# Grouping the eight attention score products of a tile in two groups of four

## What is computed

```python
q, k, v = split(shift_token(x) @ wqkv)        # 8 heads x 64
q = rotary(l2norm(q) * q_scale); k = rotary(l2norm(k) * k_scale)
# windows of 128 rows; each sees its own keys and those of the window before
sim = einsum('bhwid,bhwjd->bhwij', 8 * q, k)  # 128 x 256 per head
attn = softmax(where(mask, -max, sim))
o = einsum('bhwij,bhwjd->bhwid', attn, v)
x = x + o @ wo                                # then layer norm, w1, gelu gate, w2
```

## Time and profile before

| | |
|---|---|
| median of 3 runs | 4835.5 us |
| lowest, highest run | 4827.64, 4853.87 us |
| profiled execution, span on core 0 | 4868.1 us |
| TensorE busy | 4402.9 us, 90% of the span |
| TensorE weight loads busy (beside the products) | 2909.9 us, 60% |
| VectorE busy | 3162.0 us, 65% |
| ScalarE busy | 2817.5 us, 58% |
| GpSimd busy | 1583.5 us, 33% |
| score products, L1328 | 2048 MATMULs, 470 ns each in the mean |
| mean granted TensorE clock | 0.952 of full speed |

### The profile page before, as it was taken

How to read it: one execution, slowest core, us unless ns; L and a number is a source line. 1 busy time by engine, 2 the same in 40 slices (tenths; PEclk the granted TensorE clock), 3 DMA queues, 4 the chain that set the end, 5 groups by cost and what they waited for, 6 DMA issues and landing times.

```text
span 4868.1 us, 84300 instructions
## 1 busy us (share of the span) xinstructions
PE 4402.9 (90%) x28128; PEld 2909.9 (60%) x28128; DVE 3162.0 (65%) x8864; ACT 2817.5 (58%) x5822; POOL 1583.5 (33%) x1700
## 2 busy tenths in 40 slices
PE   8888999996999999999999999999998999999998
PEld 3444444443666666666666666666666666666666
DVE  5666666665666666666666666666666666666665
ACT  6666777674555555555555555555555555555554
POOL 2112211213333333333333333333333334333332
PEclk9999999998999999999999999999999999999999
DMA  1000000002000000000000000000000000000000
GB/s 63 28 28 28 28 19 20 19 19 83 10 9 10 9 9 9 9 10 10 10 9 9 11 9 10 10 9 9 9 9 10 9 9 9 11 9 10 9 9 6
DMA packets 71343, 74.95 MB, mean 15 GB/s; under 512 B 11792, under 2 KB 69776, under 8 KB 70288
## 3 DMA queue, kind: packets, MB, share of 16 engines
q1 hardware_dynamic: 71056, 71.88, 4.7%
HBM read 45.91 MB, written 25.17 MB: 15 GB/s over the span
## 4 chain that ended last, share of the span: by engine, by line
PE 41%; DVE 16%; issue 9%; POOL 8%; ACT 2%; DVEq 1%; DMA 0%; SPq 0%; POOLq 0%; ACTq 0%
PE f_ps L1391 16%; PE f_ps L1401 8%; POOL rnorm L946 8%; PE f_ps L1302 6%; PE f_ps L1341 4%; DVE work L1011 4%; PE f_ps L1328 4%; DVE ssq L1013 3%; DVE pr L1041 3%; DVE ssq L1015 2%; ACT qk L1198 1%; DVE hnT L1104 1%; PE f_ps L1314 1%; PE f_ps L1372 1%; POOL rstd L951 1%
## 5 line engine op out<-in xcount | busy, mean ns | idle before, releaser
L939 POOL TENSOR_TENSOR work<-qk,rot 128x256 f32<-128x256 f32 x512 | 483.7, 964 | 1227.3 <-ACT qk L1198 1213.1
L1391 PE MATMUL f_ps<-hnT,w_s 128*128 128x128 f32 (+1 forms) x6144 | 775.7, 287 | 70.4 <-DVE hnT L1104 70.4
L1391 PEld LDWEIGHTS f_ps<-hnT,w_s 128*128 128x128 f32 (+1 forms) x6144 | 727.0, 189 | 144.0 <-DVE hnT L1104 128.6
L1302 PE MATMUL f_ps<-wqkv_s,hT 128*128 128x512 f32 x1536 | 792.6, 626 | 6.0 <-ACT hT L1191 6.0
L494 ACT ACTIVATE weights<-t_ps,four_s 128x1024 f32<-128x1024 f32 (+3 forms) x768 | 631.5, 907 | 108.2 <-PE t_ps L599 104.5
L1222 ACT ACTIVATE pr<-pr,nmax,rnorm 128x256 f32<-128x256 f32 x1024 | 602.2, 589 | 111.2 <-DVE nmax L1047 106.2
L946 POOL TENSOR_TENSOR rnorm<-ssq,f_mhalf 128x8 f32<-128x8 f32 x256 | 490.1, 1914 | 196.6 <-DVE ssq L1015 182.9
L1041 DVE CUSTOM_DVE_ANT_0 pr<-f_ps,mask 128x256 f32<-128x256 f32 x1024 | 392.3, 420 | 120.3 <-PE f_ps L1328 116.5
L1328 PE MATMUL f_ps<-kT,qT 64*128 64x256 f32 x2048 | 451.3, 470 | 0.0
L1328 PEld LDWEIGHTS f_ps<-kT,qT 64*128 64x128 f32 x2048 | 298.1, 223 | 186.1 <-ACT qT L1211 127.2
L1114 DVE SCALAR_TENSOR_TENSOR act_u<-f_ps,b_s,qk 128x128 f32<-128x128 f32 (+1 forms) x768 | 222.8, 344 | 260.4 <-ACT qk L1242 258.2
(11 more groups left out here) (128 smaller groups left out, 7390.5 us busy)
## 6 DMA issues: line engine op xcount, KB each, us to landing
xs<-x_dram SPq DMA_DIRECT2D x8, 1024.0 KB, 7.8
xn_dram<-xn SPq DMA_DIRECT2D x8, 1024.0 KB, 5.3
attn_dram<-ao SPq DMA_DIRECT2D x8, 1024.0 KB, 6.2
xin<-xn_dram SPq DMA_DIRECT2D x64, 128.0 KB, 2.0
xres<-x_dram SPq DMA_DIRECT2D x64, 128.0 KB, 2.1
xres<-attn_dram SPq DMA_DIRECT2D x64, 128.0 KB, 2.1
out_dram<-yout SPq DMA_DIRECT2D x64, 128.0 KB, 1.7
wqkv_s<-wqkv_dram SPq DMA_DIRECT2D x1, 3072.0 KB, 14.6
```

The lines of the kernel that those rows point to most:

```text
L939: g.tensor_tensor(turned[s][:, heads, f], qk[s][:, heads, z], sines, ALU.mult).then_inc(turn[s], 1)
L1302: last = mm(bank(s, i), rows, wqkv_s[:, l, c, i * INNER:(i + 1) * INNER], start=(c == 0), stop=(c == KC - 1))
L1391: last = mm(bank(s, j // 2)[0:rows, o:o + P], w1_s[:, l, c, half, j * P:j * P + rows], hnT[s][:, c, :], start=(c == 0), stop=(c == KC - 1))
```

## The change

`scores` takes four heads at a time, (0, 1, 2, 3) and then (4, 5, 6, 7), so neighbours in the order alternate between the two row halves of the array and between two PSUM banks. The first group waits for kT_ready, qT_ready and v_ready at its start. score_ps goes up once per four heads; `mask_scores` waits for it before the first and third of its four parts, whose heads are now (0, 1), (2, 3), (4, 5), (6, 7); `exps` follows the same heads. In TensorE's `half`, hn_T stands between the two groups.

```diff
--- before.py
+++ after.py
@@ -823,7 +823,7 @@
         N_ROT = TILES * LAYERS
 
         STREAMS = range(2)
-        PAIRS_OF_HEADS = [(0, 2), (1, 3), (4, 6), (5, 7)]
+        QUADS_OF_HEADS = [(0, 1, 2, 3), (4, 5, 6, 7)]
         STEPS = LAYERS * PAIRS * TILES
         block = ctx.enter_context(nc.Block())
 
@@ -1032,10 +1032,11 @@
             def mask_scores(s, step, p):
 
                 n, l, it = step
-                heads = PAIRS_OF_HEADS[p]
-                both_heads = slice(heads[0], heads[1] + 1, 2)
-                dve.wait_ge(score_ps[s], n * 4 + p + 1)
-                dve.sem_inc(passed_dve, 1)
+                heads = QUADS_OF_HEADS[p // 2][p % 2 * 2:p % 2 * 2 + 2]
+                both_heads = slice(heads[0], heads[1] + 1)
+                if p % 2 == 0:
+                    dve.wait_ge(score_ps[s], n * 2 + p // 2 + 1)
+                    dve.sem_inc(passed_dve, 1)
                 for h in heads:
                     sc = bank(s, 2 * (h % 2) + h // 4)[:, (h // 2 % 2) * 256:(h // 2 % 2) * 256 + 256]
                     last = v.tensor_tensor_reduce(out=pr[s][:, h, :], in0=sc, in1=mask[s][:, 0:2 * P], scale=1.0, scalar=-3.0e38,
@@ -1218,7 +1219,7 @@
             def exps(s, step, p):
                 n, l, it = step
                 act.wait_ge(nmax_ready[s], n * 4 + p + 1)
-                for h in PAIRS_OF_HEADS[p]:
+                for h in (2 * p, 2 * p + 1):
                     last = a.activation(pr[s][:, h, :], pr[s][:, h, :], ACT.Exp, bias=nmax[s][:, h:h + 1], scale=rnorm[s][:, h:h + 1],
                                         accum_out=psum[s][:, h:h + 1])
                 last.then_inc(exped[s], 1)
@@ -1315,15 +1316,14 @@
                               qk[s][:, i * HEADS + h:i * HEADS + h + 2, :].rearrange("p h d -> p (h d)"), id_s[:, :])
                 last.then_inc(done[s], 1)
 
-            def scores(s, step, p):
-
-                n, l, it = step
-                if p == 0:
+            def scores(s, step, quad):
+
+                n, l, it = step
+                if quad == 0:
+                    pe.wait_ge(kT_ready[s], n + 1)
                     pe.wait_ge(qT_ready[s], n + 1)
-                    pe.wait_ge(kT_ready[s], n + 1)
-                if p == 1:
                     pe.wait_ge(v_ready[s], n + 1)
-                for h in PAIRS_OF_HEADS[p]:
+                for h in QUADS_OF_HEADS[quad]:
                     r = slice(h % 2 * HD, h % 2 * HD + HD)
                     last = mm(bank(s, 2 * (h % 2) + h // 4)[:, (h // 2 % 2) * 256:(h // 2 % 2) * 256 + 256], qT[s][r, h // 2, :],
                               kT[s][l][r, h // 2, :], start=True, stop=True)
@@ -1420,11 +1420,9 @@
                 heads_T(x, xs, 0, 3, qT_ps)
                 project(x, xs, 2, v_ps, (1,))
                 scores(x, xs, 0)
+                if ys:
+                    hn_T(y, ys)
                 scores(x, xs, 1)
-                if ys:
-                    hn_T(y, ys)
-                scores(x, xs, 2)
-                scores(x, xs, 3)
                 if ys:
                     up(y, ys)
                     down(y, ys)
```

More of the change, by code:

```diff
@@ L1422, in half @@
                 scores(x, xs, 0)
-                scores(x, xs, 1)
                 if ys:
                     hn_T(y, ys)
-                scores(x, xs, 2)
-                scores(x, xs, 3)
+                scores(x, xs, 1)
                 if ys:
```

## The result

The changed kernel is slower: 5064.69 us median (5042.88 to 5075.52, 4 runs) against 4844.68 us (4827.64 to 4872.84, 4 runs), a ratio of 1.0435 with a 95% interval of 1.0396 to 1.0474. Its profiled execution took 5042.88 us, the fastest of the four, with a span of 5041.1 us and a mean clock of 0.918.

A forecast was written before the change was run, and what follows sets the result against it. It took a chain of waits as the bound: the first mask delays `up` and the half. Masks 0.8 us later and 40 clock drops gave 5023 us profiled, times 0.9933 the forecast of 4990 us; range 4850 to 5095.

The forecast's parts named there:

- The first group of four: Scores on TensorE: first four heads start at 3022.90, after v, and take 1.14 us; first mask 0.83 us later, 0.8 used.
- Behind the late mask: VectorE from first mask to copy L1104 still takes 1.86 us, nothing saved; `up` starts 0.8 us later.
- The second group and the order of heads: Scores of heads 4 to 7 still take 1.14 us; reordered masks and exponentials change nothing.
- The clock: More TensorE idle time ahead of scores and `up` makes drops to 1.2 GHz more frequent; ends 4918 and 5097 us.
- n = 40: Number of clock drops chosen, between 24 and 64, in the formula of about 4843 + 4.5 n: 5023 us.
- more halves with a clock near 0.8: Sign expected in the changed profile: more of the transformer's halves slowed to a clock near 0.8.
- with 1.6 us more idle in just that place: TensorE's added idle: 0.8 us ahead of the scores, 0.8 more ahead of `up`; expected to make drops come more often.
- The factor of 0.9933: Median of runs over profiled span, 4835.5 to 4868.1; turned the profiled forecast of 5023 into 4990 us.
- Rival 1: Halves of 28.5 us instead of 27.7 change the beat of clock drops; 0 to 11 drops, 4811 us with none; chance 0.12.
- Rival 2: Score matmuls of alternating heads run one after the other, first group 0.85 us later still; median 5080 us; chance 0.09.
- Rival 3: `up` is held by something else, so the late mask costs nothing; 4835 us; chance 0.07.
- the rule weighed against rows 4: Matmuls in strict program order: alternating heads would free 0.8 us in each second group, 36 us in all; left out.

The follow-up runs named there:

- e4_fill: Kernel before with three extra unread products (1.3 us) on TensorE in the idle spell ahead of L1372: 4739.27 us, ratio 0.9754.
- e2_wait: Kernel before with only the wait for v moved ahead of the first pair of heads; pairs, order and signals kept: 5069.7 us, ratio 1.0429.
- the filled twins: The kernel before and the changed kernel, each with 1.3 us of extra products ahead of L1372 (e4_fill and e8_after_fill1): 4739.27 and 4840.4 us.
- e3_order: Kernel before with only the second group of heads in the order 4, 5, 6, 7 under one signal: 4854.37 us, ratio 0.9999.
- e8_after_fill1: Changed kernel with 1.3 us of extra unread products ahead of L1372 alone: 4840.4 us, ratio 1.0000 to the kernel before.
- e1_signal: Kernel before with score_ps signalled once per four heads; pairs, order and waits for inputs kept: 4941.26 us, ratio 1.0164.
- e7_v_late: Changed kernel with the wait for v moved from the group's first head to its second: 4940.5 us, ratio 1.0216 to the kernel before.
- e5_busy: Kernel before with four extra unread products (0.86 us) on TensorE after hnT_ready, ahead of `up`: 5076.87 us, ratio 1.049.
- e10_busy2: Kernel before with two extra unread products (0.43 us) on TensorE ahead of `up`: 4930.06 us, ratio 1.0116.
- e6_after_fill: Changed kernel with extra unread products ahead of L1372 (1.3 us), the wait for v (0.43) and `up` (0.64): 4833.42 us, ratio 0.9969 to before.

## Why the prediction was right, and where not

The forecast was 4990 us in a range of 4850 to 5095, slower with a chance of 0.83. 5064.7 lies in the range, slower, for the two reasons given, a late first mask and a lower clock; it was 75 us short.

*The first group of four.* Right in its length, 1.13 us against 1.14 taken. Its start was off by 0.1 us: "3022.90, as pair 1 did" assumed 0.05 us after the copy of v. The copy ended at 2684.18 + 0.60 = 2684.78, and the group began at 2684.93, 0.15 later. From the start of the v projection to the group it is 1.87 us, and to pair 0 it was 0.95 (e4_fill: 3004.79 to 3005.74), so the mask is 0.92 us late, not 0.83.

*Behind the late mask.* "Nothing is saved" was wrong by 0.09 us. From the first mask to the copy L1105 it now takes 2688.03 - 2686.26 = 1.77 us, against 1.86; the wait between the second and the third mask is gone. Where it is still there, in e2_wait, first and third mask are 0.98 us apart (3011.24 and 3012.22); in the changed kernel 0.89 (2686.26 and 2687.15). The two errors cancel: 0.92 - 0.09 = 0.83, and the filled twins differ by 28.47 - 27.63 = 0.84 us a half, where 0.8 was used.

*The second group and the order of heads.* Right: nothing, by e3_order.

*The clock.* The direction was right, the form was not, and that the amount nearly fits is in good part luck. The formula's end without drops holds: 4843 us, and e8_after_fill1's profiled span is 4840.8. Its n = 40 was a choice between 24 and 64 that no row priced; 5041.1 corresponds to (5041.1 - 4843) / 4.5 = 44 drops of 5.3 us. But the traces have no such drops. The kernel before had 53 stretches at 1.2 GHz, not 24, and the changed one has 106, one in most halves, most of them costing less. The sign "more halves with a clock near 0.8" did not come: below 0.85 there are 15 halves where there were 21, and the loss lies in the 76 at about 0.9.

The step that failed is the argument from idle time, "with 1.6 us more idle in just that place". Half of that time, ahead of `up`, adds nothing: e1_signal has it (1.31 us against 0.58), with no more time at 1.2 GHz than the kernel before (328 us against 345). The other half, ahead of the scores, does what was said, by e7_v_late, but only together with the spell ahead of L1372: e8_after_fill1 has both new spells and a clock of 1.00. And idle time is not the whole cause: e5_busy has as much of it as the kernel before (2.43 us of a half against 2.41), as many stretches as the changed kernel, and 553 us at 1.2 GHz. The price of a drop as a fixed 5.3 us was also only a figure that happened to serve.

*The factor of 0.9933.* This is 33 of the 75 us. It read the profiled span of before as 0.7% too long for the median. With more runs the kernel before came to 4844.7, 4848.8, 4843.1 and 4871.9 us in four comparisons. Another 24 us are the changed kernel's profile, the fastest of its four runs (5041.1 against a median of 5064.7), and only 18 the sum itself (5023 against 5041.1). Three runs and one profile don't fix such a factor.

*Rival 1* (the clock falls out of step and the kernel gains) had the right idea, that the length of the half matters, and the wrong result: with the spell ahead of L1372 left open, every longer half had more stretches (69 to 121 against 53), and at best a little less time at 1.2 GHz (317 us in e10_busy2 against 345). *Rival 2* (no overlap) is out by 1.13 us for eight matmuls. *Rival 3* (delay taken up) is out by the 1.32 us wait of `up`. On the rule weighed against rows 4, that matmuls start and end in program order (the Trainium skill, "TensorE: Matmul & The Clock Gate", "The mechanism"): e2_wait and the changed kernel take the same 2.08 us with different orders of heads, so nothing here was freed by alternating them, as rows 4 said.

## What to carry to other kernels

Before reordering work to make neighbours overlap, see in the timeline whether they overlap already; here the stretch of eight at 1.14 us said so, and the new order brought only its price, a joint wait and a coarser signal. A product that waits for less than its group must not be made to wait for the group: two matmuls let through early were worth 106 to 124 us here. And where TensorE's granted clock is below 1.00 in a periodic kernel, price any change of the period with and without the longest idle spell filled, because the clock's part can be nearly as large as the change's own.

## What the hardware showed that was not expected

Extra products whose results nobody reads made the kernel before 2.5% faster (4739.27 us, ratio 0.9754, 0.9725 to 0.9783), by raising the transformer's mean clock from 0.95 to 1.00. In the changed kernel the same edit gave 5064.7 to 4840.4 us.

A longer half cost far more than its length over part of the range: going from 0.43 to 0.86 us of extra work added 147 us over 128 halves by the medians, 181 by the ratios and 141 in the traces, where 55 would be its length. Without new idle time, the same step took the time at 1.2 GHz from 317 to 553 us.

TensorE began the score products 0.15 us after the releasing copy when it stood idle with nothing else to do, and 0.05 us after it when it was still busy with pair 0. In e6_after_fill, where an extra product shortens the idle time ahead of the same wait to 0.16 us, the scores start 1.77 us after the v projection's start in place of 1.86.
